# Adding the two halves of K on POOL instead of the Vector engine, in the Sinkhorn attention of a one-core kernel

## The reference, cut to what matters

```python
C = 1.0 - jnp.einsum('bhnd,bhmd->bhnm', qn, qn)
C = jnp.where(eye, DIAG_VAL, C)
log_K = -C / OT_REG
for _ in range(SINKHORN_ITERS):           # 10
    log_u = log_marg - jax.nn.logsumexp(log_K + log_v[..., None, :], axis=-1)
    log_v = log_marg - jax.nn.logsumexp(log_K + log_u[..., :, None], axis=-2)
z = jnp.exp(log_u[..., :, None] + log_K + log_v[..., None, :])
z = z / jnp.max(z, axis=(-2, -1), keepdims=True)
z = jnp.where(eye, 1.0, z)
attn = jax.nn.softmax(z * scale, axis=-1)
out = jnp.einsum('bhnm,bhmd->bhnd', attn, v)
```

## Time and profile before

| | |
|---|---|
| median of 3 runs | 5643.05 us (5639.24 to 5648.45) |
| time of the profiled execution | 5627.77 us, span 5626.0 us |
| mean granted TensorE clock | 0.899 of full speed |
| PE busy | 4651.3 us, 83% |
| DVE busy | 4007.4 us, 71% |
| ACT busy | 3109.6 us, 55% |
| POOL busy | 837.1 us, 15% |
| DVE on `join` (L899) | 459.8 us in 384 instructions |

### The profile page before, as it was taken

One profiled execution on the slowest core, in us unless ns is written; L12 is line 12 of the kernel. 1 busy time (PEld: TensorE's weight loads), 2 busy tenths in 40 slices (PEclk: granted clock), 3 DMA queues, 4 the chain that ended last, 5 costly groups with the idle time before them and its releaser, 6 DMA issues. The chain is left out here.

```text
span 5626.0 us, 198571 instructions
## 1 busy us (share of the span) xinstructions
PE 4651.3 (83%) x84786; PEld 3606.0 (64%) x84787; DVE 4007.4 (71%) x8485; ACT 3109.6 (55%) x4426; POOL 837.1 (15%) x394
## 2 busy tenths in 40 slices
PE   4667766766859999999999999999999469699960
PEld 3445544544428888888888888888888335477740
DVE  8889889886536777777777777777787644355545
ACT  4566666664335666665666666666665323277740
POOL 2444444443000000000000000000000013300027
PEclk9888888888879999999999999999999676699985
DMA  1000000000320000000000000000000222222223
GB/s 57 25 25 13 25 25 13 25 25 17 103 49 14 15 21 15 21 15 15 21 15 21 15 21 15 20 16 15 21 15 9 82 66 76 86 68 69 65 63 109
DMA packets 186921, 198.18 MB, mean 35 GB/s; under 512 B 86848, under 2 KB 167040, under 8 KB 183552
## 3 DMA queue, kind: packets, MB, share of 16 engines
q1 hardware_dynamic: 173824, 160.79, 9.6%
q0 software_dynamic: 12288, 25.18, 1.5%
HBM read 123.00 MB, written 62.91 MB: 33 GB/s over the span
## 5 line engine op out<-in xcount | busy, mean ns | idle before, releaser
L643 PE MATMUL y_ps<-k_sb,x_sb 128*12 128x256 f16 x58368 | 1705.6, 275 | 21.5 <-DVE x_sb L880 13.0
L643 PEld LDWEIGHTS y_ps<-k_sb,x_sb 128*12 128x12 bf16 x58368 | 1433.4, 88 | 209.9 <-issue 38.7
L257 PE MATMUL acc<-w_hl,feat_h 128*128 128x384 f16 x3456 | 642.0, 350 | 424.5 <-DVE h_sb L203 299.3
L762 ACT ACTIVATE y_sb<-y_ps 128x256 f32<-128x256 f32 x912 | 347.6, 381 | 920.9 <-PE y_ps L643 920.9
L257 PEld LDWEIGHTS acc<-w_hl,feat_h 128*128 128x128 f16 x3456 | 356.1, 104 | 685.6 <-issue 370.3
L150 POOL TENSOR_TENSOR feat_l<-work,feat_h 128x2048 f16<-128x2048 f32 x96 | 576.3, 6003 | 778.5 <-ACT feat_h L241 739.8
L771 ACT ACTIVATE k_new<-cos,k_bias 128x512 f32<-128x512 f32 x768 | 520.3, 682 | 166.5 <-PE cos L670 166.4
L653 PEld LDWEIGHTS turned_x<-rows_in,y_sb 128*128 128x128 f32 x3648 | 478.1, 191 | 118.9 <-issue 71.6
L911 DVE CUSTOM_DVE_ANT_0 plan<-plan,u_rows,v_last 128x512 f32<-128x512 f32 x768 | 535.2, 744 | 4.1
L653 PE MATMUL turned_x<-rows_in,y_sb 128*128 128x16 f32 x3648 | 527.0, 258 | 8.6 <-ACT y_sb L762 8.4
L241 ACT ACTIVATE feat_h<-work 128x4096 f16<-128x4096 f32 x96 | 388.2, 4044 | 201.5 <-PE acc L264 199.4
(11 more groups left out here) (253 smaller groups left out, 7286.5 us busy)
## 6 DMA issues: line engine op xcount, KB each, us to landing
xt<-in_x_dram SPq DMA_DIRECT2D x16, 1280.0 KB, 5.8
x_in_sb<-expert_rows SPq DMA_DIRECT2D x39, 384.0 KB, 3.2
expert_results<-y_sb SPq DMA_DIRECT2D x39, 384.0 KB, 2.5
q_left<-q_parts SPq DMA_DIRECT2D x192, 64.0 KB, 2.9
q_right<-q_parts SPq DMA_DIRECT2D x192, 64.0 KB, 2.9
v_parts<-v_sb SPq DMA_DIRECT2D x16, 408.0 KB, 2.4
v_in_sb<-v_parts SPq DMA_DIRECT2D x48, 136.0 KB, 3.3
h_tokens<-h_sb SPq DMA_DIRECT2D x16, 384.0 KB, 2.5
```

Source lines behind the costliest of these rows:

```text
L257: nc.tensor.matmul(acc[a][:, q, 0:2 * DIM], block_of, w_hl[:, k, :, :].rearrange("p a d -> p (a d)"), start=(k == 0), stop=False)
L643: last = nc.tensor.matmul(y[a][32 * c:32 * c + XW, :, :], high[:, j, XW * h:XW * (h + 1)], k_sb[s][:, h, :, at:at + P], start=(h == 0 and ...
```

## The change

POOL gets a loop over the phases of its own and makes `join` of all four heads of group G - 2 there: four additions of 512 columns for each head in place of DVE's two of 1024. The waits are the same, with one on `k_built` (the low part of that head is written), which DVE didn't need, being its writer. `joined` is signalled by the last of the four. On DVE, `join` and its four calls go. Everything else is as before.

```diff
+            def join(F, s, h):
+                H = F * GH + h
+                after(pool, k_built, F * GH + h + 1)
+                after(pool, pv_ready, H - 1)
+                for c in range(TB):
+                    cols = slice(c * TOKENS, (c + 1) * TOKENS)
+                    last = nc.gpsimd.tensor_tensor(plan[h % 2][:, c, :], k_sb[s][:, h, 0, cols], k_sb[s][:, h, 1, cols], ALU.add)
+                last.then_inc(joined, 1)
+
+            def phase(G, t, s, young=False, old=False, build=False, fin=False, tail=False):
+                if fin:
+                    for h in range(GH):
+                        join(G - 2, (s + 1) % 3, h)
+
+            phases(pool, phase)
...
-            def join(F, s, h, half):
-                H = F * GH + h
-                if half == 0:
-                    after(dve, pv_ready, H - 1)
-                cols = slice(half * 2 * TOKENS, (half + 1) * 2 * TOKENS)
-                done = nc.vector.tensor_tensor(plan[h % 2][:, 2 * half:2 * half + 2, :].rearrange("p b n -> p (b n)"),
-                                               k_sb[s][:, h, 0, cols], k_sb[s][:, h, 1, cols], ALU.add)
-                if half == 1:
-                    done.then_inc(joined, 1)
...
                         if fin:
-                            join(G - 2, new, a, 0)
-                            join(G - 2, new, a, 1)
                             times_u(G - 2, new, a, (0, 1))
                     if c == 1 and fin:
                         times_u(G - 2, new, a, (2, 3))
-                        join(G - 2, new, b, 0)
                     if c == 2:
                         if build:
                             low_parts(G, new, a)
-                        if fin:
-                            join(G - 2, new, b, 1)
```

## The result

The changed kernel takes 5760.24 us (median of 4 runs, 5755.78 to 5766.07) against 5643.73 for the kernel before in the same comparison: ratio 1.0207, 95% interval 1.0189 to 1.0225. That is 116.5 us slower. The forecast was 5713 us, 70 us slower, in a range of 5634 to 5800: the direction and the mechanism hold, the size was two fifths short.

The account below looks back on a forecast made before the run. PE bounds the kernel, DVE only through its slack. 45 x 0.77 + 31 x 1.13 = 70 us; 5627.8 + 70 = 5698 profiled, 15.3 more for the runs' median: 5713. Range 5634 to 5800.

Parts of the forecast that it names:

- Exclusion, turns and price: POOL and DVE instructions reading two SBUF tensors shut each other out, alternating; a 512-column piece takes 1.18 us alone; chance 0.54.
- the custom operation is untouched: L911, one tensor in SBUF, isn't shut out; rival that it is: some 0.8 us x 90 more, 5785, chance 0.06.
- fits in the slack: Rival: a piece takes under 0.8 us, so PE's chain is unchanged: 5643 us, chance 0.15.
- L894 never lasts four pieces: Rival: POOL gives DVE no turn between pieces, so four block for 4.72 us: 178 us lost, 5821, chance 0.14.
- Faster: Rival: in the last two finishing phases, where PE waits for head_max, up to 20.2 us come back: 5623, chance 0.11.
- Odd heads: nothing: Joins of odd heads run undisturbed until L878, which waits some 0.1 us, within the slack of 0.22.
- The second half phase: Even head's join there delays the old group's split, so PE starts 0.77 us late, in 45 phases.
- The first half phase: Even head's join there delays low part and splits; the old multiply starts 1.13 us late, counted 31 times.
- At the loop's back edge: First half phase's loss is absorbed in 13 passages, where PE stalls anyway, up to 3.2 us, 2.9 in the mean.
- The end of the attention: Joins leave DVE's queue but take about 4.5 us on POOL where they took 2.35; counted as nothing.
- the forecast's upper bound, 5778: Without any start-up hidden, the two losses are 1.63 and 1.99 us, in all 135 us.
- The lower bound's 30 us: Smallest loss in the forecast's own case, lock by turns with 30 to 135 us lost; its own range starts at 5673.

Follow-up runs that it names:

- POOL only writes: Changed kernel with the join left out, POOL writing constants by eight memsets a head behind the same waits: 5653.05 us, 0.9990 of the kernel before.
- second profile of the changed kernel: The changed kernel run again, unaltered, on another chip: 5750.69 us, 1.0196 of the kernel before.
- join after the first split: Changed kernel with POOL's first join of each phase waiting for the new group's first split: 5721.18 us, 1.0118 of the kernel before.
- the delays alone: Kernel before, nothing on POOL, with two memsets in DVE's order that make two splits late in each full phase: 5727.50 us, 1.0167.

## Why the prediction was right, and where it was short

**What bounds the kernel** was read rightly: PE, and DVE only through its slack. The kernel whose POOL only writes takes DVE's 460 us away and gains nothing.

**Exclusion, turns and price** held: a piece takes 1.157 us in the median (1.18 taken), L896 behind a whole piece 1.08, the custom operation is untouched. The rivals fall: no piece is under 1.139 us, so nothing fits in the slack; L894 never lasts four pieces; the custom operation keeps its 744 ns. "Faster" fails at the place it named: at the end of the attention the last intervals get longer.

**Odd heads: nothing** held in the steady state (55.7 us with these alone on POOL).

**The second half phase:** 0.65 to 0.78 us, 0.70 in the mean, against 0.77.

**The first half phase** is the step that failed. The prediction said that the old multiply could start at 3062.09, 1.13 us late, and didn't ask who comes before it. But the young multiply of cycle 1 waits for `first_x`, the split of the row sums at the end of the phase before. The working had that split's end, 3060.69; with 0.06 for the semaphore and PE's old start of 3059.13, it gives 1.62 us; 1.63 was measured. 45 x 0.77 + 31 x 1.62 = 85 us in place of 70. At the loop's back edge this loss is absorbed, as forecast: in the second profile of the changed kernel the 13 passages have 61.99 us in the mean, 0.56 more than before, less than the second half phase's 0.70 alone.

**The end of the attention,** counted at nothing, costs 10.6 us; the kernel with DVE's join there gets 9.6 back. The prediction looked there at the length of the join alone, 4.5 us for 2.35. That length costs nothing, as the kernel that only writes shows; what costs are the splits that the join holds up, in a stretch where PE had no slack for them, and the clock.

**What remains:** with the measured losses the steady state gives 45 x 0.70 + 31 x 1.63 = 82 us, and 113.7 - 82 - 10.6 = 21. In size that is TensorE's clock: four of the 31 intervals are 1.6 us longer than their neighbours, and six of the 13 with the back edge stand at 64.7 to 65.1 us, where the others are at 61.0 to 62.3; the kernel before has one such (64.1). 4 x 1.6 + 5 x 2.9 = 21 us. Only the first term goes with the change. The second profile of the changed kernel has six of the longer 31 but one of the long 13, and 100.7 us in all; the kernel that only writes has one of the 13 as well. In one of the four the multiplies took 5.33 us for 3.67, and the windows have the clock at half, 1.2 GHz of 2.4, between 1799 and 1801 us, behind a wait of 1.56 us:

```profile
1797.11 5.33 PE L643 MATMUL y_ps<-k_sb,x_sb 128*12 128x256 f16 x128 [1.56 <-DVE x_sb L896]
```

```profile
1795.00:1797.00 2.00, 0.55 (x6) 0.45 (x5) 1.93 (x4) 2.00 (x5) 2.00 (x3) 1.00 0.00 0
1797.00:1799.00 2.00, 1.89 (x52) 1.54 (x56) 1.90 (x8) 1.39 (x2) 1.12 (x2) 0.75 0.00 0
1799.00:1801.00 2.00, 2.00 (x48) 1.47 (x40) 1.22 (x4) 0.38 (x1) 0.00 (x0) 0.50 0.03 8
1801.00:1803.00 2.00, 2.00 (x49) 1.53 (x42) 0.00 (x0) 0.38 (x1) 0.00 (x0) 0.90 0.00 0
```

That the long waits bring this about is likely and not settled. For it: in the kernel before the clock is below full in 12 of the 13 intervals with the back edge, where PE stalls for up to 3.2 us, and in none of the other 34; the four kernels with no wait for DVE above 0.7 us (odd heads, only writes, 256 columns, join after the first split) have no such interval among their 31, and the four with waits of 1.5 us have two to six and the one with 2.9 us nearly all; the delays alone bring it too, without POOL. Open is why only some of the equal waits do.

**Luck:** 5760 lies under the forecast's upper bound, 5778, but not for the bound's reason. That one stood for start-ups that don't hide in the wait, and they do: a subtraction behind a piece needs its few hundredths of a microsecond. The bound happened to cover the step that was missing. The lower bound's 30 us have no working of their own in the prediction.

No version here beats the kernel before, and there is nothing measurable to gain this way: taking the join from DVE at no cost was the kernel that only writes.

## What to carry to other kernels

Before work goes to an idle engine, look for instructions of the relieved one that share something with it, and lay their times beside the moved work; here two engines read SBUF with two tensors each, and 0.19-us instructions on the critical chain took up to 1.1 us. Cut the moved work into short pieces and start it in a stretch without such instructions: with the same work, pieces of 2048, 512 and 256 columns cost 240, 116 and 46 us. List for each late instruction all who wait for it, the next phase's first consumer too. And when a cost agrees with its forecast, look whether another kernel has the supposed cause without the cost, as here at the end of the attention.

## What the runs showed of the hardware

- POOL's memsets, which read nothing, don't disturb DVE's operations with two SBUF inputs at all (189 and 2274 ns, as alone), while its additions hold them up for a whole instruction.
- An addition of two f16 tensors into f32 on POOL takes 669 ns for 256 columns, 1157 for 512 and 4068 for 2048 (medians): 0.18 to 0.19 us and 1.9 ns a column, about as much as the 4.18 us with an f32 input.
- Waits of PE of 1.5 us and more cost more than their length when TensorE's clock falls to half behind them: 1.6 us on top in four to six phases of 31 in the changed kernel, and 1.2 to 2.8 us on top of 4.5 in most phases of the one with a single piece.
- DVE's reciprocals (258 ns) and its custom operation with one tensor in PSUM (744 ns) keep their times beside POOL's additions.
